# A four-layer transformer program: the masked attention's engines in another order, the key bias as one row, and half of the gate sigmoids computed again

## The chip, the cores and the metric

The program runs on one core of one Trainium2 chip. The metric is the device time in microseconds (us), median of the runs shown; shorter is better. Five engines work side by side, each through its own list of instructions, and meet at semaphores: TensorE (PE in the profile), VectorE (DVE), ScalarE (ACT), GpSimd (POOL) and SyncE (SP), which here issues nearly all DMA transfers.

## The reference, cut to what matters

Two layers follow each other over `x` of 16 sequences x 256 tokens x 512. The first layer is a cross-attention and a gated feed-forward part with quantized activations; the second a masked attention and a feed-forward part with LoRA experts. The change touches the quantized part and the masked attention. In short form, with names of this text:

```
# quantized feed-forward (x1 -> x2)
gate, up  = qdq16(xq @ w_gate.T), qdq16(xq @ w_up.T)      # 16-bit, one scale per tensor: its largest value
sig       = min(round(sigmoid(gate) * 65536), 65535) / 65536
act       = qdq16(gate * sig)                              # scale from the largest |gate * sig|
out       = qdq16(act * up)                                # scale from the largest |act * up|
x2        = x1 + out @ w_down.T

# masked attention (x2 -> x3), one head of width 512; q from layernorm(x2), k from ctx
proj(z)   = (z @ W1.T + b1) @ W2.T + b2
p         = softmax(proj(layernorm(x2)) @ proj(ctx).T / sqrt(512) + mask)   # mask is (256, 256), one for all sequences
x3        = x2 + p @ ctx
```

The kernel folds both projections into one 512 x 512 matrix, so the scores are `norm(x2) @ keys + t + mask`. `keys` is a 512 x 256 array of each sequence. `t` is one number of each key and the same for all queries; it is the key bias of the title.

## The kernel before

Matrices are handled as a high part and a low part in a reduced float format (fp32r), and each product is three matmuls (lines 183 to 185, `product`). The stages run one after the other, each a block with its own tiles; tiles are named by stage: `at_` cross-attention, `pg_` and `pu_` the gate and up projections, `om_` the pass that finds the largest output, `dn_` the down projection, `ma_` the masked attention, `lf_` the last feed-forward part.

**`pu_` (`project`).** 96 tiles of 128 x 512, twelve for each of eight chunks of 512 tokens. For each tile ScalarE takes the sigmoid, VectorE rounds it to 16 bits (`pu_sq`, line 1366), and SyncE stores it to memory (line 1293) and stores the raw up projection beside it.

**`om_` (`output_maximum`).** 48 pieces n of 128 x 1024, six for each chunk. SyncE loads raw up values (512 KB, `om_raw`) and rounded sigmoids (256 KB, `om_sq`). VectorE multiplies gate and sigmoid (`om_prod`, line 1636), ScalarE turns it into the 16-bit `act` in place (line 1576), VectorE multiplies by up (`om_outp`, line 1643) and reduces to the largest (line 1647). Beside this chain the same engines make the keys and key biases of the masked attention. TensorE turns and multiplies; ScalarE takes results out of PSUM (`om_craw`, `om_rout`); GpSimd splits the context in two parts (lines 1673 and 1675), and adds each chunk's bias to the mask for two groups of 128 queries (`key_biases`, line 1682, sixteen adds of 128 x 512 in all). The result, mask plus bias, is stored as `bias_d`, 256 KB for each sequence. GpSimd closes the stage with `partition_all_reduce` (line 1717), which gives the scale that the next stage needs.

**`ma_` (`masked_attention`).** Sequence b passes through: statistics of x2 (DVE), the power for 1/deviation (POOL, line 2007), the shift (DVE, line 2046), normalization (ACT, line 2100), a transposition on TensorE (line 2160), its high part (ACT, 2107) and low part (DVE, 2050), the scores (24 matmuls of 256 columns), the bias and mask and row maximum (DVE `logits`, 2058), the exponentials (ACT, 2128), the transposition of the probabilities (PE, 2181), their parts (ACT 2136, DVE 2063), the product with the values (12 matmuls of 512 columns), and the output (DVE, 2076). Keys and values are split on ACT (2113, 2119) and POOL (2011, 2015). No planner is involved: each engine runs a loop over steps s, written by hand, in which each call carries an offset such as `s + 1` or `s - 2`. The order of the calls in that loop body, and the offsets, are the order of the work.

## Time and profile before

| what | us |
|---|---|
| median of 3 runs | 3729.22 (3728.66 to 3734.64) |
| the profiled execution's own time | 3723.7 |
| its span | 3721.9 |
| PE, DVE, ACT, POOL busy in it | 3253.1, 1929.0, 1532.9, 859.2 |
| granted TensorE clock, mean | 0.942 of full speed |

The span is what the profiler saw; the 1.8 us around it are start and end. The page gives busy time as a share of the whole span, and this program has stages with quite different limits, so the shares are read for one stage at a time. The chain of waits on the page ends in the `lf_` stage and says nothing about the stages of the change.

### The profile page before, as it was taken

The numbers are of one execution on the slowest core, as the hardware profiler recorded it, in microseconds if no ns is written. First come the engines' busy times: TensorE is split into PE (matmuls) and PEld (weight loads), VectorE is DVE, ScalarE is ACT, GpSimd is POOL, SyncE is SP. The second block draws the span as 40 slices with busy tenths as digits, with TensorE's granted clock in tenths as the row PEclk, the third lists the DMA queues.
The fourth block names the chain that finished last, engine by engine and source line by source line (L and its number), as shares of the span: only waits on it lengthen the run. The fifth ranks groups of instructions, "written<-read, shape, count | busy, mean of one in ns | idle before, by whom it ended". The sixth has DMA issues, their size and how long they took to land. (4 is left out here: it accounts for less than half of the span.)

```text
span 3721.9 us, 51622 instructions
## 1 busy us (share of the span) xinstructions
PE 3253.1 (87%) x17272; PEld 2789.6 (75%) x17272; DVE 1929.0 (52%) x3245; ACT 1532.9 (41%) x2915; POOL 859.2 (23%) x1149
## 2 busy tenths in 40 slices
PE   7999899999999969999997859975545999999998
PEld 6998788888888858877874648865533778777776
DVE  3355477777777745557898865534433222222221
ACT  3222276666666633326775656534422111111110
POOL 0000076666766720000004530004310000000000
PEclk9999999999999979999997879997876999999999
DMA  6577654544554435546777874434431001110000
GB/s 178 161 231 231 208 155 141 146 143 141 147 150 133 132 111 206 183 152 226 241 251 232 273 259 158 164 137 151 156 118 62 32 23 34 35 34 32 22 33 12
DMA packets 385410, 524.33 MB, mean 141 GB/s; under 512 B 60435, under 2 KB 245011, under 8 KB 380767
## 3 DMA queue, kind: packets, MB, share of 16 engines
q1 hardware_dynamic: 372424, 512.11, 43.5%
q0 software_dynamic: 2176, 8.39, 0.6%
q10 hardware_dynamic: 10592, 1.04, 0.2%
q8 instruction: 125, 2.05, 0.2%
q14 instruction: 93, 0.75, 0.1%
HBM read 303.29 MB, written 184.55 MB: 131 GB/s over the span
## 5 line engine op out<-in xcount | busy, mean ns | idle before, releaser
L2378 DVE SCALAR_TENSOR_TENSOR lf_hT<-lf_hb,lf_hT 128x512 fp32r<-128x512 f32 x128 | 88.5, 692 | 630.1 <-ACT lf_hT L2436 628.6
L2436 ACT ACTIVATE lf_hT<-lf_hb 128x512 fp32r<-128x512 f32 x128 | 76.6, 598 | 690.6 <-PE lf_py L185 641.7
L766 POOL TENSOR_TENSOR at_prob<-at_prob,at_rec 128x308 f32<-128x308 f32 (+1 forms) x256 | 261.7, 1045 | 265.1 <-DVE at_rec L808 264.8
L901 ACT ACTIVATE at_prob<-at_sc,at_nm 128x77 f32<-128x77 f32 (+1 forms) x1024 | 293.5, 383 | 41.8 <-DVE at_nm L795 41.7
L795 DVE TENSOR_REDUCE at_nm<-at_sc 128x4 f32<-128x308 f32 (+1 forms) x256 | 164.6, 685 | 172.7 <-PE at_sc L955 172.7
L914 ACT ACTIVATE at_pT<-at_tp 128x1024 fp32r<-128x1024 f32 x128 | 131.6, 1028 | 202.1 <-PE at_tp L965 202.1
L183 PE MATMUL lf_hb<-lf_xT,lf_w 128*128 128x512 f32 x512 | 204.1, 399 | 0.0
L184 PE MATMUL lf_hb<-lf_xT,lf_w 128*128 128x512 f32 x512 | 202.5, 395 | 0.0
L184 PE MATMUL lf_py<-lf_w,lf_hT 128*128 128x512 f32 x512 | 202.5, 395 | 0.0
L185 PE MATMUL lf_py<-lf_w,lf_hT 128*128 128x512 f32 x512 | 202.4, 395 | 0.0
L185 PE MATMUL lf_hb<-lf_xT,lf_w 128*128 128x512 f32 x512 | 202.4, 395 | 0.0
L183 PE MATMUL lf_py<-lf_w,lf_hT 128*128 128x512 f32 x512 | 202.3, 395 | 0.0
L183 PE MATMUL dn_py<-qf_wd,dn_om 128*128 128x512 f32 x384 | 150.1, 391 | 38.1 <-DVE dn_om L1858 38.1
L801 DVE TENSOR_REDUCE at_sums<-at_prob 128x4 f32<-128x308 f32 (+1 forms) x256 | 172.7, 675 | 0.0
L183 PE MATMUL pg_bank<-pg_xs,qg_wg 128*128 128x512 f32 x384 | 153.5, 400 | 20.3 <-DVE pg_xs L1359 20.3
L2318 POOL TENSOR_SCALAR lf_var<-lf_mv 128x1 f32<-128x1 f32 x32 | 7.2, 224 | 703.4 <-DVE lf_mv L2331 703.4
L753 POOL TENSOR_TENSOR at_ks<-at_kr,at_ks 128x512 fp32r<-128x512 f32 x128 | 164.8, 1288 | 14.4 <-ACT at_ks L908 14.4
L812 DVE TENSOR_TENSOR at_pT<-at_tp,at_pT 128x1024 fp32r<-128x1024 f32 x128 | 156.1, 1220 | 22.5 <-ACT at_pT L914 22.4
L183 PE MATMUL pu_bank<-pu_xs,qu_wu 128*128 128x512 f32 x384 | 151.0, 393 | 18.1 <-DVE pu_xs L1359 17.5
L183 PE MATMUL at_vq<-at_xT,xo_Wq 128*128 128x256 f32 x512 | 146.9, 287 | 17.4 <-DMA at_xT<-xn_parts 12.6
L183 PE MATMUL at_vq<-at_pT,at_vs 128*128 128x256 f32 x512 | 156.5, 306 | 1.0 <-DVE at_oT L818 0.8
L955 PE MATMUL at_sc<-at_ks,at_qs 128*128 128x256 f32 x1024 | 148.5, 289 | 5.3 <-DMA at_qs<-at_qst 5.2
(315 smaller groups left out, 9635.8 us busy)
## 6 DMA issues: line engine op xcount, KB each, us to landing
at_kr<-k_rows SPq DMA_DIRECT2D x256, 128.0 KB, 2.8
at_qs<-at_qst SPq DMA_DIRECT2D x512, 64.0 KB, 2.0
raw_gate<-pg_stage SPq DMA_DIRECT2D x96, 256.0 KB, 2.0
pu_rg<-raw_gate SPq DMA_DIRECT2D x96, 256.0 KB
raw_up<-pu_stage SPq DMA_DIRECT2D x96, 256.0 KB, 2.1
om_raw<-raw_up SPq DMA_DIRECT2D x48, 512.0 KB, 4.3
dn_raw<-raw_up SPq DMA_DIRECT2D x48, 512.0 KB, 3.8
xn_parts<-pr_xturned SPq DMA_DIRECT2D x32, 512.0 KB, 4.9
```

The source lines that it names most:

```text
L183: pe.matmul(out, lh, rh, start=start, stop=False, **kw)
L184: pe.matmul(out, lh, rl, start=False, stop=False, **kw)
L185: return pe.matmul(out, ll, rh, start=False, stop=stop, **kw)
L753: pool.tensor_tensor(ks[:, n % NK, :, 1, :], kr[:, n % NKR], ks[:, n % NK, :, 0, :].bitcast(F32), ALU.subtract).then_inc(k_low, 1)
L766: ins = pool.tensor_tensor(prob[:, i, :, lo:hi], prob[:, i, :, lo:hi], rec[:, z, g, :].unsqueeze(2).broadcast_to([P, 2 * NTE, hi - lo]), A ...
L795: ins = dve.tensor_reduce(nm[:, n % 2, g, :], sc[n % 2][:, :, lo:hi], AX_X, ALU.max, negate=True)
L801: dve.tensor_reduce(sums[:, z, g, :], prob[:, i, :, SEG[g][0]:SEG[g][1]], AX_X, ALU.add).then_inc(sum_done, 1)
L812: dve.tensor_tensor(pT[:, n % 2, 1], tp[:], pT[:, n % 2, 0].bitcast(F32), ALU.subtract).then_inc(pt_done, 1)
L901: ins = act.activation(prob[:, i, m, lo:hi], sc[n % 2][:, m, lo:hi], ACT.Exp, bias=nm[:, n % 2, g, m:m + 1])
L914: act.activation(pT[:, n % 2, 0], tp[:], ACT.Copy).then_inc(pt_hi, 1)
L955: ins = pe.matmul(sc[n % 2][:, h * NTE + m, :], qs[:, n % NQ, h, m * P:(m + 1) * P], ks[:, n % NK, h, part, :], start=part == 0, stop=part ...
L2378: dve.scalar_tensor_tensor(hT[:, i, 1, :], hb[i][:], 0.0, hT[:, i, 0, :].bitcast(F32), ALU.max, ALU.subtract).then_inc(h_done, 1)
```

## The change

Four parts.

1. **The bias as one row.** `output_maximum` no longer adds the bias to the mask. ScalarE writes the 512 biases of a chunk as one row on one partition, SyncE stores 2 KB for a chunk, and the mask is not loaded there. The masked attention loads the mask once and all biases once (one row of 16 x 256), and TensorE adds the bias to the scores by a matmul of a column of ones with the row: two for each sequence, in plain float32.
2. **Half of the sigmoids.** Pieces with even n of the `om_` pass compute the sigmoid again (ScalarE) and round it again (VectorE, `rounded`). `pu_` stores, and `om_` loads, only those with odd n.
3. **The masked attention's loops.** On each engine the calls come in another order with other offsets, and the outputs are taken one step later (LAG_Y = 3). More buffers: ten for x, three for raw and split keys, four for values.
4. Small: a memset of ones at the start of GpSimd's list in `ma_`; other places for some tiles of `om_`; the last key bias stored one step sooner.

```diff
-                        if gate is not None:
+                        if gate is not None and j % 4 > 1:
                             wait_alone(sp, sq_done, KF * c + j + 3, spacer_s)
                             sp.dma_start(sq_d[...], sq[:, j % 2, :]).then_inc(sq_stored[j % 2], 16)
...
-                    sp.dma_start(sq[:, n % 2, :], part(sq_d, n // SUB, n % SUB)).then_inc(sq_ready[n % 2], 16)
+                    if n % 2:
+                        if n >= 2:
+                            sp.wait_ge(prod_done, n - 1)
+                        sp.dma_start(sq[:, 1, :], part(sq_d, n // SUB, n % SUB)).then_inc(sq_ready, 16)
...
+                def sigmoid(n):
+                    if n >= 2:
+                        act.wait_ge(sq_done, n // 2)
+                    act.activation(sig[:], place(n), ACT.Sigmoid, scale=scal[:, S_G:S_G + 1]).then_inc(sig_ready, 1)
...
-                    act.activation(trow, tb[:], ACT.Identity, bias=bb[:, 0:1]).then_inc(t_out, 1)
+                    act.activation(trow[:, c % 2, :], tb[0:1, :], ACT.Identity, bias=bb[0:1, 0:1]).then_inc(t_out, 1)
+                sigmoid(0)
+                sigmoid(2)
                 for n in range(N):
                     products(n)
+                    if n % 2 and n + 3 < N:
+                        sigmoid(n + 3)
...
+                def rounded(n):
+                    dve.wait_ge(sig_ready, n // 2 + 1)
+                    if n >= 2:
+                        dve.wait_ge(prod_done, n - 1)
+                    dve.tensor_scalar(sq[:, 0, :], sig[:], SIGQ, SIGQ - 1, ALU.mult, ALU.min).then_inc(sq_done, 1)
...
                 for n in range(N):
+                    if n % 2 == 0 and n + 2 < N:
+                        rounded(n + 2)
                     outputs(n)
...
-                for c in range(NCH):
-                    if c + 1 < NCH:
-                        context(2 * c + 2)
-                    if c:
-                        key_biases(c - 1)
-                    if c + 1 < NCH:
-                        context(2 * c + 3)
-                key_biases(NCH - 1)
+                for x in range(2, 2 * NCH):
+                    context(x)
                 pool.wait_ge(row_max, 1)
                 pool.partition_all_reduce(big[:, 0:1], mx_row[:], P, RMAX).then_inc(all_max, 1)
...
-    LEAD_X, LEAD_R, LAG_T, LAG_V = 1, 2, 1, 2
-    NX, NR, NB_ = 8, 2, 3
+    LAG_V, LAG_Y = 2, 3
+    NX, NR, NC, NT_, NB_ = 10, 3, 2, 3, 4
...
# VectorE's loop body of the masked attention
             for s in range(FIRST, LAST + 1):
-                if 0 <= s + LEAD_X < B:
-                    turned_x(s + LEAD_X)
+                if 0 <= s - LAG_Y < B:
+                    outputs(s - LAG_Y)
+                if 0 <= s + 1 < B:
+                    turned_x(s + 1)
+                if 0 <= s + 2 < B:
+                    offset(s + 2)
                 if 0 <= s + 3 < B:
                     statistics(s + 3)
-                if 0 <= s - LAG_T < B:
-                    turned_low(s - LAG_T)
-                    reciprocals(s - LAG_T)
-                if 0 <= s - LAG_V < B:
-                    outputs(s - LAG_V)
                 if 0 <= s < B:
                     logits(s)
-                if 0 <= s + 3 < B:
-                    offset(s + 3)
+                if 0 <= s - 1 < B:
+                    turned_low(s - 1)
+                    reciprocals(s - 1)
# ScalarE's
-                if 0 <= s + LEAD_X < B:
-                    turned_x(s + LEAD_X)
-                if 0 <= s - LAG_T < B:
-                    turned_high(s - LAG_T)
-                if 0 <= s + LEAD_R < B:
-                    keys_high(s + LEAD_R)
+                if 0 <= s + 1 < B:
+                    turned_x(s + 1)
+                if 0 <= s + 2 < B:
+                    keys_high(s + 2)
                 if 0 <= s + 1 < B:
                     values_high(s + 1)
-                if 0 <= s + 3 < B:
-                    normalized(s + 3)
+                if 0 <= s + 2 < B:
+                    normalized(s + 2)
+                if 0 <= s - 1 < B:
+                    turned_high(s - 1)
                 if 0 <= s < B:
                     exps(s)
# TensorE's
+                    pe.matmul(sc[b % 2][:, t, :], ones[:], trow[:, b, :], start=True, stop=False)
                     for k in range(KD):
                         ins = product(...)
...
-                if 0 <= s + LEAD_X < B:
-                    turn_x(s + LEAD_X)
-                if 0 <= s - LAG_T < B:
-                    turn(s - LAG_T)
+                if 0 <= s + 1 < B:
+                    turn_x(s + 1)
                 if 0 <= s < B:
                     scores(s)
+                if 0 <= s - 1 < B:
+                    turn(s - 1)
                 if 0 <= s - LAG_V < B:
                     values(s - LAG_V)
```

What the engines then execute, at three places. First TensorE in the middle of `ma_`, where a step begins (the four probabilities' transpositions are `ma_tp`, the scores `ma_sc`, the values' product `ma_po`). Before:

```order
L185 MATMUL ma_po<-ma_val,ma_pT 128x512
L2160 MATMUL ma_xtp<-ident,ma_xn 128x128 x8
L2181 MATMUL ma_tp<-ident,ma_prob 128x128 x4
L183 MATMUL ma_sc<-ma_rT,ma_xT 128x256
L184 MATMUL ma_sc<-ma_rT,ma_xT 128x256
```

and after:

```order
L185 MATMUL ma_po<-ma_val,ma_pT 128x512
L2166 MATMUL ma_xtp<-ident,ma_xn 128x128 x8
L2176 MATMUL ma_sc<-ma_trow,ma_ones 128x256
L183 MATMUL ma_sc<-ma_rT,ma_xT 128x256
...
L185 MATMUL ma_sc<-ma_rT,ma_xT 128x256
L2188 MATMUL ma_tp<-ident,ma_prob 128x128 x4
L183 MATMUL ma_po<-ma_val,ma_pT 128x512
```

The transposition of the probabilities moved from ahead of the scores to behind them, and a bias matmul stands ahead of each half of the scores.

Then one whole step of VectorE in `ma_`, before:

```order
L2050 TENSOR_TENSOR ma_xT<-ma_xtp,ma_xT 128x1024
L2030 BN_STATS ma_st<-ma_y 128x6 x2
L2035 BN_AGGR ma_mv<-ma_st 128x2 x2
L2040 TENSOR_SCALAR ma_var<-ma_mv 128x2
L2063 TENSOR_TENSOR ma_pT<-ma_tp0,ma_pT 128x512
L2069 RECIPROCAL ma_rec<-ma_sums 128x2
L2076 SCALAR_TENSOR_TENSOR ma_y<-ma_po,ma_rec,ma_y 128x512 x2
L2058 ISA ma_logit,ma_nm<-ma_sc1,ma_bias 128x256
L2058 ISA ma_nm 128x1
L2058 ISA ma_logit,ma_nm<-ma_sc1,ma_bias 128x256
L2058 ISA ma_nm 128x1
L2046 SCALAR_TENSOR_TENSOR ma_shift<-ma_mv,ma_rstd 128x2
```

and after:

```order
L2082 SCALAR_TENSOR_TENSOR ma_y<-ma_po,ma_rec,ma_y 128x512 x2
L2056 TENSOR_TENSOR ma_xT<-ma_xtp,ma_xT 128x1024
L2052 SCALAR_TENSOR_TENSOR ma_shift<-ma_mv,ma_rstd 128x2
L2036 BN_STATS ma_st<-ma_y 128x6 x2
L2041 BN_AGGR ma_mv<-ma_st 128x2 x2
L2046 TENSOR_SCALAR ma_var<-ma_mv 128x2
L2064 ISA ma_logit,ma_nm<-ma_sc0,ma_mask 128x256
L2064 ISA ma_nm 128x1
L2064 ISA ma_logit,ma_nm<-ma_sc0,ma_mask 128x256
L2064 ISA ma_nm 128x1
L2069 TENSOR_TENSOR ma_pT<-ma_tp1,ma_pT 128x512
L2075 RECIPROCAL ma_rec<-ma_sums 128x2
```

The outputs moved ahead of the step (and are those of one sequence earlier); the shift moved from behind the logits to behind the low part of the turned x.

Last, the end of GpSimd's list in `om_`; the first of the two ISA rows has no semaphore to wait for. Before:

```order
L1673 CAST qf_wd<-om_craw 128x4x256
L1675 TENSOR_TENSOR qf_wd<-om_craw,qf_wd 128x4x256
L1682 TENSOR_TENSOR qf_fold<-qf_fold 128x512 x4
L1717 ISA
L1717 ISA big<-om_mx_row 128x1
```

and after:

```order
L1694 CAST qf_wd<-om_craw 128x4x256
L1696 TENSOR_TENSOR qf_wd<-om_craw,qf_wd 128x4x256
L1724 ISA
L1724 ISA big<-om_mx_row 128x1
L1497 UNCONDITIONAL_BRANCH
```

The adds of mask and bias are gone, here the last four.

## Rows read from the trace of the kernel before

**Rows 1.** Busy time in three stages: stretch, its length, engines, clock, DMA share, GB/s.
```profile
460.00:1387.00 927.00, 825.03 (x6037) 776.62 (x6036) 655.50 (x1220) 589.54 (x1603) 605.93 (x929) 0.97 0.47 138
...
1960.00:2215.00 255.00, 187.02 (x760) 139.70 (x760) 207.46 (x150) 150.07 (x167) 116.36 (x64) 0.83 0.81 262
...
2500.00:2760.00 260.00, 147.67 (x768) 132.37 (x768) 112.91 (x240) 98.73 (x161) 86.59 (x48) 0.76 0.42 146
```
**Rows 2.** Scores of `ma_`, by tile: ns min/median/max, first and last start.
```profile
L185 PE MATMUL ma_sc<-ma_rT,ma_xT x128: 274/415/415, 2529.1 to 2738.8; 128*128 128x256 f32 x128
```
**Rows 3.** One step of `ma_` in order of time: start, duration, engine, [idle before, releaser].
```profile
2583.65 1.12 PE L2181 MATMUL ma_tp<-ident,ma_prob 128*128 128x128 f32 x4 [5.39 <-ACT ma_prob L2128]
...
2584.42 0.56 PE L183 MATMUL ma_sc<-ma_rT,ma_xT 128*128 128x256 f32 x1
...
2585.68 1.28 DVE L2030 BATCH_NORM_STATS2 ma_st<-ma_y 128x6 f32<-128x512 f32 x2
...
2587.12 0.28 PE L183 MATMUL ma_sc<-ma_rT,ma_xT 128*128 128x256 f32 x1
...
2587.91 0.69 DVE L2063 TENSOR_TENSOR ma_pT<-ma_tp,ma_pT 128x512 fp32r<-128x512 f32 x1 [0.24 <-issue]
...
2588.55 0.39 PE L183 MATMUL ma_po<-ma_val,ma_pT 128*128 128x512 f32 x1
...
2591.36 1.04 PE L2160 MATMUL ma_xtp<-ident,ma_xn 128*128 128x128 f32 x8
2591.56 1.41 DVE L2076 SCALAR_TENSOR_TENSOR ma_y<-ma_po,ma_rec,ma_y 128x512 f32<-128x512 f32 x2 [2.88 <-PE ma_po L185]
...
2592.76 2.34 POOL L2015 TENSOR_TENSOR ma_val<-ma_cin,ma_val 128x1024 fp32r<-128x1024 f32 x1 [0.42 <-ACT ma_val L2119]
...
2593.57 1.55 DVE L2046 SCALAR_TENSOR_TENSOR ma_shift<-ma_mv,ma_rstd 128x2 f32<-128x2 f32 x1
...
2595.24 1.52 ACT L2100 ACTIVATE ma_xn<-ma_y,ma_shift,ma_rstd 128x512 f32<-128x512 f32 x2 [2.56 <-DVE ma_shift L2046]
...
2597.64 1.00 ACT L2107 ACTIVATE ma_xT<-ma_xtp 128x1024 fp32r<-128x1024 f32 x1
...
2597.79 1.11 PE L2181 MATMUL ma_tp<-ident,ma_prob 128*128 128x128 f32 x4 [5.40 <-ACT ma_prob L2128]
...
2598.68 1.23 DVE L2050 TENSOR_TENSOR ma_xT<-ma_xtp,ma_xT 128x1024 fp32r<-128x1024 f32 x1 [3.56 <-ACT ma_xT L2107]
```
**Rows 4.** The shift of `ma_`, by line: ns min/median/max.
```profile
L2046 DVE SCALAR_TENSOR_TENSOR ma_shift<-ma_mv,ma_rstd x16: 156/1547/2199, 2517.7 to 2709.1; 128x2 f32<-128x2 f32 x16
```
**Rows 5.** Matmuls whose operands are plain float32 (two records for each), by line.
```profile
L1752 PE MATMUL om_rb<-qf_fold x32: 592/592/1061, 2004.1 to 2018.8; 128*128 128x512 f32 x32
```
**Rows 6.** Rounding of a sigmoid tile in `pu_`, by tile.
```profile
L1366 DVE TENSOR_SCALAR pu_sq<-pu_sig x96: 415/417/430, 1684.0 to 1953.1; 128x512 uint16<-128x512 f32 x96
```
**Rows 7.** `om_`, by line: count, busy us, mean ns, idle us before and releaser.
```profile
L1636 DVE TENSOR_TENSOR om_prod<-qf_gate,om_sq 128x1024 f32<-128x1024 int16 x48 | 80.1, 1670 | 29.4 <-DMA om_sq<-gate_sigmoids 29.4
L1643 DVE TENSOR_TENSOR om_outp<-qf_gate,om_up 128x1024 f32<-128x1024 int16 x48 | 74.9, 1561 | 7.0 <-DVE om_mx L1647 1.0
L1647 DVE TENSOR_REDUCE om_mx<-om_outp 128x1 f32<-128x1024 f32 x48 | 58.0, 1208 | 0.1
...
L1682 POOL TENSOR_TENSOR qf_fold<-qf_fold 128x512 f32<-128x512 f32 x16 | 27.7, 1754 | 21.1 <-DMA key_biases<-qf_fold 13.5 <-ACT qf_fold L1597 7.7
```
**Rows 8.** VectorE in `om_`: two starts of `om_prod`, four pieces apart.
```profile
2100.59 3.10 DVE L1636 TENSOR_TENSOR om_prod<-qf_gate,om_sq 128x1024 f32<-128x1024 int16 x1 [2.35 <-DMA om_sq<-gate_sigmoids]
...
2122.31 3.18 DVE L1636 TENSOR_TENSOR om_prod<-qf_gate,om_sq 128x1024 f32<-128x1024 int16 x1 [2.61 <-DMA om_sq<-gate_sigmoids]
```
**Rows 9.** The end of `om_` in order of time.
```profile
2201.40 0.20 DVE L1657 TENSOR_REDUCE om_mx_row<-om_mx 128x1 f32<-128x48 f32 x1
2202.01 2.48 POOL L1682 TENSOR_TENSOR qf_fold<-qf_fold 128x512 f32<-128x512 f32 x2 [13.46 <-DMA key_biases<-qf_fold]
...
2210.41 0.38 POOL L1717 PARTITION_ALL_REDUCE big<-om_mx_row  x1 [5.92 <-issue]
```

More of the change, by code:

```diff
@@ L1444, in output_maximum @@
         raw_ready = [ph.sem(f"raw_ready{i}") for i in range(2)]
-        sq_ready = [ph.sem(f"sq_ready{i}") for i in range(2)]
+        sq_ready, sig_ready, sq_done = ph.sem("sq_ready"), ph.sem("sig_ready"), ph.sem("sq_done")
         up_ready, prod_done, gate_ready, out_done, max_done = (
@@ L1463, in output_maximum @@
         cT = [wd[:, :, 2 * KD:3 * KD, :], wd[:, :, KD:2 * KD, :]]
-        mask = w2[:, 0, :].rearrange("p (q s) -> p q s", q=NK)
-        trow = w2[:, 1, :]
-        bias = w2[:, 2:4, :]
+        trow = w2[0:1, 0:2, :]
+        gb = wd[:, 1, 2:4, :].rearrange("p a (k n) -> p a k n", k=KD)
         betas = rout[:, 0, :].rearrange("p (k n) -> p k n", k=KD)
@@ L1471, in output_maximum @@
         tb = ph.ps("tb", [P, CT])
[L1472 removed]
+        w2_ready, w1_ready, b_ready, c_ready = (ph.sem(n) for n in ("w2_ready", "w1_ready", "b_ready", "c_ready"))
         turned, turned_out, m_full, m_out, beta_full, beta_out, g_full, g_out, gc_full, gc_out = (
@@ L1520, in store_bias @@
                 def store_bias(c):
-                    sp.wait_ge(bias_done, NK * c + NK)
-                    for b in range(NB):
-                        sp.dma_start(bias_d[NB * c + b], bias[:, :, b * S:(b + 1) * S]).then_inc(bias_stored, 16)
+                    sp.wait_ge(t_out, c + 1)
+                    sp.dma_start(bias_d[c:c + 1, :], trow[:, c % 2, :]).then_inc(t_stored[c % 2], 16)
                 def load_down(parts, ks):
@@ L1539, in _ @@
                     if n == 6:
-                        sp.wait_ge(turned, KD)
-                        sp.dma_start(mask, a["fside_1xSxS2_0"].rearrange("o (m p) s -> p (o m) s", p=P)).then_inc(mask_ready, 16)
                         load_context(1)
@@ L1546, in _ @@
                         store_keys(*keys_due(n - 3))
-                    if bias_due(n - 4) is not None:
-                        store_bias(bias_due(n - 4))
+                    if bias_due(n - 3) is not None:
+                        store_bias(bias_due(n - 3))
                     if n == 24:
@@ L1551, in _ @@
                         load_down((0,), (0, KD))
-                for n in range(N, N + 8):
+                for n in range(N, N + 4):
                     if keys_due(n - 3):
@@ L1557, in _ @@
                         load_down((0, 1), (2 * KD, 3 * KD))
-                    if bias_due(n - 4) is not None:
-                        store_bias(bias_due(n - 4))
-                sp.wait_ge(bias_stored, 16 * B)
+                    if bias_due(n - 3) is not None:
+                        store_bias(bias_due(n - 3))
+                sp.wait_ge(t_full, NCH)
+                for s in t_stored:
+                    sp.wait_ge(s, 16 * NCH // 2)
                 load_down((1,), (0, KD))
-                sp.wait_ge(t_full, NCH)
                 load_down((0, 1), (KD, 2 * KD))
@@ L1675, in context @@
                     pool.tensor_tensor(cT[c % 2][:, 1, :, lo:lo + S], craw[:], cT[c % 2][:, 0, :, lo:lo + S].bitcast(F32), ALU.subtract).then_inc(c_low, 1)
-                def key_biases(c):
-                    pool.wait_ge(t_out, c + 1)
-                    if c:
-                        pool.wait_ge(bias_stored, 16 * NB * c)
-                    for q in range(NK):
-                        pool.tensor_tensor(bias[:, q, :].rearrange("p (b s) -> p b s", b=NB), mask[:, q, :].unsqueeze(1).broadcast_to([P, NB, S]),
-                                           trow.rearrange("p (b s) -> p b s", b=NB), ALU.add).then_inc(bias_done, 1)
                 pool.memset(betas, 1.0).then_inc(cleared, 1)
@@ L1703, in _ @@
                 pool.wait_ge(gbraw_done, 1)
+                pool.wait_ge(turned, KD)
                 pool.tensor_copy(gb[:, 0], gbraw).then_inc(gb_hi, 1)
@@ L1923, in masked_attention @@
         rraw = ph.sb("rraw", [P, NR, KD, S])
-        rT = ph.sb("rT", [P, 2, 2, KD, S], F32R)
-        cin = ph.sb("cin", [P, NR, NK, D])
+        rT = ph.sb("rT", [P, NT_, 2, KD, S], F32R)
+        cin = ph.sb("cin", [P, NC, NK, D])
         val = ph.sb("val", [P, NB_, 2, NK, D], F32R)
-        bias = ph.sb("bias", [P, NB_, NK, S])
+        mask = ph.sb("mask", [P, NK, S])
+        trow = ph.sb("trow", [1, B, S])
+        ones = ph.sb("ones", [1, P])
         logit = ph.sb("logit", [P, 2, NK, S])
@@ L1965, in load_values @@
             def load_values(b):
[L1966 to L1973 removed]
+                if b >= NC:
+                    sp.wait_ge(v_low, b - NC + 1)
+                sp.dma_start(cin[:, b % NC], rows(ctx_in, b)).then_inc(c_ready[b % NC], 16)
             def store(b):
@@ L1998, in _ @@
             for i in range(NX):
-                sp.wait_ge(stored[i], 16 * (B // NX))
+                sp.wait_ge(stored[i], 16 * len(range(i, B, NX)))
         @block.gpsimd
@@ L2057, in logits @@
                 for t in range(NK):
-                    dve.tensor_tensor_reduce(logit[:, b % 2, t, :], sc[b % 2][:, t, :], bias[:, b % NB_, t, :], -1.0, 3.0e38, ALU.add, ALU.min,
+                    dve.tensor_tensor_reduce(logit[:, b % 2, t, :], sc[b % 2][:, t, :], mask[:, t, :], -1.0, 3.0e38, ALU.add, ALU.min,
                                              nm[:, b % 2, t:t + 1]).then_inc(max_done, 1)
```

87 lines of the change are left out of this document (43 added, 44 removed).

## The prediction

> **What bounds the kernel now.** I read the busy time by stage first, since the whole-span shares mix stages. In `ma_` (260 us) TensorE is busy 148 us, VectorE 113, ScalarE 99, GpSimd 87 [rows 1]: no engine is even at 60%, the DMA share is 0.42, and the clock is 0.76 of full. So this stage is bound by a circle of waits. `om_` (255 us) is different: VectorE is busy 207 us and the DMA share is 0.81 [rows 1]. The stages before, between and after are left as they are or are bound by TensorE.
>
> The timeline of one step shows the circle [rows 3]. TensorE ends its step with the values' product and the transposition of x at about 2592.4, then idles 5.4 us until the exponentials of the same step are there. These wait in ScalarE's list behind the normalization, that waits 2.56 us for the shift, and the shift stands behind VectorE's outputs and logits, which come after TensorE's last matmul. So TensorE (2583.65 to 2592.4), VectorE (2591.56 to 2595.12) and ScalarE (2595.24 to 2597.64) work in turn: one step is 14.1 us here. Over the stage, sixteen steps' scores run from about 2528.7 to 2738.8 [rows 2]; less the last block of scores, about 4.5 us, that is 205 us for 15 steps, 13.7 us each.
>
> Two things make the circle longer than its work. Behind the 5.4 us of idle, the clock is low: the first 12 score matmuls take 2.70 us (2584.42 to 2587.12), the next 12 take 1.43 us [rows 3], so 1.3 us a step. And the shift, two numbers for each partition, takes 1.55 us, where its shortest is 0.156 us [rows 3, 4]. It starts at 2593.57 inside GpSimd's subtraction (2592.76 to 2595.10) and ends 0.02 us after it: it was held by that subtraction.
>
> **The masked attention, step by step.** After the change the transposition of the probabilities is behind the scores, and the outputs are those of three steps back, so each engine has work of other sequences in hand. Then the longest single list, or a shorter circle, sets the step.
>
> TensorE, at the pace of full clock: x turned 1.04; scores 24 x 0.119 = 2.86; values from 2588.55 to 2591.36, 2.81; probabilities turned, half of x's, 0.5 [rows 3]. Added are the two bias matmuls. A plain float32 matmul leaves two records, 592 ns each at 512 columns, against 390 ns for an fp32r one [rows 5, 3]. The 256-column records of rows 3 take 0.28 for 0.119 of pace, so about 0.16 is latency; 0.43 for 512 columns, 0.215 for 256, and four records are 0.86 us a step. The bounds are 0.24 us (two records at the fp32r pace) and twice 0.86 at the low clock. I take 0.86, the nearest row. Sum: 8.1 us.
>
> VectorE: outputs and logits 2.01 (2591.56 to 2593.57), low part of x 1.23, statistics 2.0 (2585.68 to 2587.91, less 0.24 of waiting), low part of the probabilities 0.69, shift and reciprocal 0.16 each [rows 3, 4]. Sum 6.25 us, if nothing holds it.
>
> Now who waits for whom, counted from the end of a shift. VectorE: statistics to 2.0, logits to 2.7, probabilities and reciprocal to 3.55, outputs to 4.9. ScalarE: normalization to 1.5, the high part of the probabilities to 2.1, the exponentials wait for the logits and run 2.8 to 3.8, then the high part of x to 4.8 (normalization and exponentials are 2.40 together, the high part 1.00 [rows 3]). VectorE's low part of x: 4.9 to 6.1. In the meantime ScalarE did the high part of the next keys, another 1.0, to about 5.8, and GpSimd's subtraction for them starts at 5.9, just ahead of the shift. The subtraction takes 2.34 (as the one for the values [rows 3]), so the shift ends at 8.3 to 8.4. With some tenths for semaphores and one small VectorE operation that may be held by the second subtraction, 8.7 us a step. That is above TensorE's 8.1, so TensorE idles about 0.6 us a step. In the cross-attention it is busy 825 of 927 us (89%) and the clock is 0.97 [rows 1]; so I take full clock.
>
> The trace shows that the shift was held, and nothing of VectorE with an operand in PSUM. The Trainium skill, "SBUF — State Buffer", section "Who interferes with whom", says that VectorE with two SBUF inputs and GpSimd reading SBUF exclude each other for the whole instruction, whoever starts first. By that rule the trace agrees, and the shift is the only large risk in the list above: the outputs, the low parts and the logits each read one operand from PSUM. If the lock fell otherwise (shift first), the step would be TensorE's 8.1; that is the first rival.
>
> Saved: 15 x (13.7 - 8.7) = 75 us. The start stays: GpSimd's first power comes late there and the two transpositions and first scores still follow it. The added wait of TensorE, for mask and bias row, is ahead of its whole list, but both loads are issued with the first x and land while it waits for the power anyway. The end gets shorter, since the last exponentials and transposition no longer wait for a normalization or a transposition ahead of them: about 4 us, between 0 and 8. Memory traffic is four transfers of 0.52 MB a step; at 8.7 us 241 GB/s, less than the 262 of `om_` [rows 1], so I cost it at nothing; if that cover is gone, the step grows (a rival).
>
> **The pass for the largest output.** Removed from GpSimd: 16 adds, 27.7 us [rows 7]. They count by what they hold on VectorE. `om_prod` has a mean of 1670 ns and `om_outp` 1561; the unheld ones take about 1220, nearly the reduction's 1208, which is never held [rows 7]. So VectorE is held (450 + 341) ns x 48 = 38 us, by all of GpSimd's work; the adds are a quarter of its 116 us, 8 to 9 us. Also removed: for the second half of the pass, half of the sigmoid loads and 4 MB of bias stores. VectorE waits 29.4 us for sigmoids [rows 7]; once every four pieces it is 2.4 to 2.6 us, at 21.7 us for four [rows 8]. Some 15 us of the 29.4 lie at the start, where the weights' loads are in front and one odd piece still needs its load: 1 us less. Of the rest I take half, 7 us; bounds 0 and 15.
>
> Added on VectorE: 24 roundings of 1024 columns. The row shows 417 ns for 512 [rows 6]; twice that, 0.83, is the upper end, and 0.417 plus half a reduction's slope (0.27), 0.68, the value taken, as 417 is less than the reduction needs for 512 columns. 24 x 0.68 = 16 us on the engine that bounds the pass, the last rival doubling it. The Trainium skill's same section says that a `tensor_scalar` can take the second port pair too and then excludes GpSimd. No row here shows one beside GpSimd; by that rule a rounding can be held for a whole subtraction, up to 2.4 us, by the other it is never held. I add 4 us, in between. Sigmoids on ScalarE, 24 of at least 1.0 us (its operations of 1024 columns in rows 3), run in the 105 us in which it is idle [rows 1]. Loop: -8 - 7 - 1 + 16 + 4 = +4 us; bounds -16 and +30.
>
> The tail gains. VectorE has its row maximum at 2201.6; GpSimd then still does the last adds (it waited 13.46 us for a store to free the tile) and ends at 2204.5; the all-reduce starts 5.92 us behind that, waiting for nothing shown [rows 9]. After the change nothing but the earlier context work stands ahead, and the ISA row that precedes the all-reduce has no wait, so these 5.9 us pass long before. The scale comes at about 2202.3 instead of 2210.8: 8 us, and `dn_` starts with it, if its loads follow; bounds 0 and 9. In `pu_` TensorE bounds, and the halved stores change nothing.
>
> **Sum.** -75 - 4 + 4 - 8 = -83 us. On the profiled execution's 3723.7 us: 3641. The median of the runs, 3729.2, is 5.5 above it, and one of the three runs is another 5 above; I forecast the median: 3646 us.
>
> **The rivals.**
> - *The shift is not held.* ScalarE's keys come later or the shift slips in first; the step is TensorE's 8.1: 15 x 0.6 = 9 us less, 3637. For it: the race is decided by 0.2 us. Against: at 8.1 the circle has little slack.
> - *The clock dips in each step.* TensorE's short idles bring back the 1.3 us of rows 3: 9.4 a step, +10 us, 3656.
> - *Another wait in `ma_`.* Loads that now come at 241 GB/s, or a buffer freed late (values have only two raw ones, keys three), hold a step at 11 us: +35 us, 3681. For it: loads are issued by one queue behind stores. Against: most are issued a step ahead.
> - *The pass gets worse.* Roundings cost the upper price and are held, and the idle for loads stays: +30 instead of +4, 3672.
> - *Slower than before.* TensorE stays at the low clock, as behind its idles now: its list is then twice 8.1, 16.2 us a step, against 13.7: 15 x 2.5 = +38, with -4 - 4 for the rest, 3759. It decides from a mean step of 14.3 us on. Against: TensorE would then never idle, and in rows 3 the clock rose after 3 us of unbroken work.
> - *The order doesn't loosen the circle.* The step stays at 13.7; only the other parts count, -4 us or so: 3725.
>
> **How the numbers follow.** Forecast (8.4 to 9.0 a step) 40%; shift not held 17%; clock dips 14%; other wait 13%; pass worse 9%; slower 4%; circle stays 3%. The likeliest is 3646. The range 3624 to 3685 takes in the first five but their ends: below, the unheld shift with the pass's lower bound; above, the slow loads. About 0.2% (7.5 us) is what a measurement of this kernel can tell from no change: faster 0.94, same 0.02, slower 0.04.
>
> **What would show it.** In the changed profile: the `ma_` stage near 180 us with a clock above 0.9; the wait of TensorE for the exponentials gone; a shift with a median near 2 us, and starts of it 8.7 us apart; bias matmuls as four records a step. In `om_`: no GpSimd adds, the all-reduce under 1 us behind VectorE's last reduction, roundings of 0.7 us, and VectorE's wait for sigmoids near 15 us. I am wrong if the step is over 9.7 us, or if `om_` grows by more than 15 us.

## The result and the profile after

The changed kernel takes 3639.31 us (median of 4 runs, 3638.54 to 3642.45) against 3728.94 us for the kernel before (4 runs, 3722.93 to 3734.64): a ratio of 0.9761, 95% interval 0.9745 to 0.9778. The profiled execution took 3638.5 us, with a span of 3636.9 and a mean clock of 0.953. The forecast was 3646 us, so the time was right within 7 us, and 4.7 of these come from the 5.5 us added for the median, which lies only 0.8 us above the profiled execution here. By its number alone the result is nearer to the rival "the shift is not held" (3637 us); the trace decides against that rival, since every shift was held. The reason was right for the largest part and wrong in one step that happened to cost little.

Where the 85 us between the two spans (3721.9 and 3636.9) lie, by starts of named instructions in the two traces:

| stretch | before | after | change | forecast |
|---|---|---|---|---|
| up to VectorE's row maximum in `om_` | 2201.40 | 2198.20 | -3.2 | +4 |
| from there to the first product of `dn_` | 22.8 | 16.3 | -6.5 | -8 |
| from there to the first statistics of `ma_` | 280.3 | 281.5 | +1.3 | 0 |
| `ma_`, first statistics to last output | 251.4 | 173.3 | -78.2 | -79 |
| the rest | 965.9 | 967.6 | +1.6 | 0 |

Busy time in the two stages of the change, then in 60 us of steady `ma_` steps (stretch, length, PE, PEld, DVE, ACT, POOL, clock, DMA share, GB/s); it answers to [rows 1]:

```profile
1955.00:2205.00 250.00, 182.78 (x760) 136.87 (x760) 223.92 (x183) 174.97 (x191) 86.33 (x50) 0.85 0.71 225
2490.00:2675.00 185.00, 146.64 (x832) 119.15 (x832) 130.18 (x240) 96.38 (x161) 87.06 (x49) 0.87 0.53 184
...
2560.00:2620.00 60.00, 60.00 (x365) 49.15 (x364) 57.22 (x107) 41.65 (x72) 38.10 (x21) 1.00 0.74 248
```

The last row is the surprise. TensorE is busy all of 60 us at full clock, and VectorE 57.2 of them. The prediction had VectorE set the step and TensorE idle 0.6 us of it.

One step of the changed `ma_` in order of time, answering to [rows 3] (start, duration, engine, instruction, [idle before, releaser]):

```profile
2578.29 2.40 POOL L2016 TENSOR_TENSOR ma_rT<-ma_rraw,ma_rT 128x1024 fp32r<-128x1024 f32 x1 [2.87 <-ACT ma_rT L2119]
2578.45 2.26 DVE L2052 SCALAR_TENSOR_TENSOR ma_shift<-ma_mv,ma_rstd 128x2 f32<-128x2 f32 x1
...
2580.05 0.60 PE L2188 MATMUL ma_tp<-ident,ma_prob 128*128 128x128 f32 x4
...
2583.28 1.03 PE L2166 MATMUL ma_xtp<-ident,ma_xn 128*128 128x128 f32 x8
...
2584.25 0.69 PE L2176 MATMUL ma_sc<-ma_trow,ma_ones 1*128 1x256 f32 x2
...
2586.49 0.69 PE L2176 MATMUL ma_sc<-ma_trow,ma_ones 1*128 1x256 f32 x2
...
2586.97 2.25 DVE L2052 SCALAR_TENSOR_TENSOR ma_shift<-ma_mv,ma_rstd 128x2 f32<-128x2 f32 x1
...
2588.66 0.60 PE L2188 MATMUL ma_tp<-ident,ma_prob 128*128 128x128 f32 x4
```

No row of TensorE has an idle in front: the wait of 5.39 us for the exponentials is gone. TensorE's step is 2580.05 to 2588.66, 8.61 us; VectorE's (one shift to the next) is 8.52. The shift starts 0.16 us behind GpSimd's subtraction of the keys (2578.29 to 2580.69) and ends with it (2580.71), as the prediction had it. Half of the scores takes 2584.25 to 2586.49, 2.24 us; 12 score matmuls at 0.119 are 1.43, so a bias matmul takes 0.81 us out of the list and not 0.43. That is 0.8 us a step more than priced. From start to start the list is 0.96 for turning x, 4.41 for the scores with both biases, 0.36 for turning the probabilities and 2.88 for the values: 8.6 us.

All sixteen shifts, answering to [rows 4]:

```profile
L2052 DVE SCALAR_TENSOR_TENSOR ma_shift<-ma_mv,ma_rstd x16: 2185/2254/2264, 2509.8 to 2638.2; 128x2 f32<-128x2 f32 x16
```

The first of them lies in the start of the stage. Before the change it was not held, now it is:

```profile
2517.69 0.16 DVE L2046 SCALAR_TENSOR_TENSOR ma_shift<-ma_mv,ma_rstd 128x2 f32<-128x2 f32 x1 [11.16 <-POOL ma_rstd L2007]
```
```profile
2509.80 2.19 DVE L2052 SCALAR_TENSOR_TENSOR ma_shift<-ma_mv,ma_rstd 128x2 f32<-128x2 f32 x1 [11.72 <-POOL ma_rstd L2012]
```

`om_` by line, answering to [rows 7] (count | busy us, mean ns | idle before, releaser):

```profile
L1654 DVE TENSOR_TENSOR om_prod<-qf_gate,om_sq 128x1024 f32<-128x1024 int16 x48 | 91.3, 1903 | 12.4 <-DMA om_sq<-gate_sigmoids 12.4
L1661 DVE TENSOR_TENSOR om_outp<-qf_gate,om_up 128x1024 f32<-128x1024 int16 x48 | 64.9, 1353 | 3.3
...
L1644 DVE TENSOR_SCALAR om_sq<-om_sig 128x1024 uint16<-128x1024 f32 x24 | 17.6, 734 | 3.5 <-ACT om_sig L1572 3.5
```

And the end of `om_`, answering to [rows 9]:

```profile
2198.20 0.20 DVE L1678 TENSOR_REDUCE om_mx_row<-om_mx 128x1 f32<-128x48 f32 x1
2198.54 0.38 POOL L1724 PARTITION_ALL_REDUCE big<-om_mx_row  x1 [23.05 <-DVE om_mx_row L1678]
2198.96 0.16 DVE L1681 TENSOR_TENSOR scal<-scal 128x1 f32<-128x1 f32 x1 [0.55 <-POOL big L1724]
...
2213.35 1.15 ACT L1841 ACTIVATE dn_up<-dn_raw,scal 128x1024 int16<-128x1024 f32 x1 [18.08 <-DMA dn_raw<-raw_up]
2214.53 1.23 DVE L1863 TENSOR_TENSOR dn_prod<-qf_gate,dn_up 128x1024 f32<-128x1024 int16 x1 [14.54 <-ACT dn_up L1841]
```

The all-reduce follows the row maximum by 0.34 us, where it took 9.0 before. The scale is there 8.7 us earlier relative to the maximum; `dn_` takes 6.5 of them. In both traces its first operation waits for a load last, and from the issue of that load to the operation it is 6.3 us before (2216.79 to 2223.06) and 8.9 us after (2204.43 to 2213.35).

### The profile page after: what moved, and what is told of

It reads as the page before. It is cut to its first block and busy times, and to the rows that moved or that the text cites. A ratio compares the mean times of both kernels' runs of the same rounds, so it can differ in the third digit from the quotient of the medians.

```text
span 3636.9 us, 51541 instructions
## 1 busy us (share of the span) xinstructions
PE 3247.5 (89%) x17336; PEld 2773.5 (76%) x17336; DVE 1961.0 (54%) x3269; ACT 1554.9 (43%) x2939; POOL 828.2 (23%) x1134
## 5 line engine op out<-in xcount | busy, mean ns | idle before, releaser
L753 POOL TENSOR_TENSOR at_ks<-at_kr,at_ks 128x512 fp32r<-128x512 f32 x128 | 164.8, 1288 | 16.2 <-ACT at_ks L908 16.2
L812 DVE TENSOR_TENSOR at_pT<-at_tp,at_pT 128x1024 fp32r<-128x1024 f32 x128 | 156.1, 1220 | 22.8 <-ACT at_pT L914 22.8
```

Source lines behind the costliest of these rows:

```text
L753: pool.tensor_tensor(ks[:, n % NK, :, 1, :], kr[:, n % NKR], ks[:, n % NK, :, 0, :].bitcast(F32), ALU.subtract).then_inc(k_low, 1)
L812: dve.tensor_tensor(pT[:, n % 2, 1], tp[:], pT[:, n % 2, 0].bitcast(F32), ALU.subtract).then_inc(pt_done, 1)
```

## The experiments

Theory T, read off the trace above: TensorE's list of 8.6 us sets the step. Theory V, the prediction's: VectorE's list with the held shift does. Each kernel was timed beside the kernel before; ratios are compared, and 0.001 is 3.7 us. One ratio is known to about 0.0015, so a difference of two below 0.002 (8 us) is not clear of noise; where such a small one is read below, it rests on the traces. "`ma_`" is the time from the start of the first statistics to the start of the last pair of outputs in its trace. A step is taken from one first transposition of the probabilities to the next, in the steady part of the stage; for the two kernels whose steps differ much the mean of all 15 stands.

| kernel | median us | ratio, 95% interval | `ma_` us | steady step us |
|---|---|---|---|---|
| before | 3723.3 to 3730.6 | 1 | 251.4 | 13.4 mean |
| changed | 3639.3 | 0.9761 (0.9745 to 0.9778) | 173.3 | 8.61 |
| changed, again | 3638.9 | 0.9759 (0.9741 to 0.9776) | 173.7 | 8.61 |
| bias in fp32r, 64 rows | 3634.5 | 0.976 (0.9747 to 0.9774) | 172.1 | 8.51 |
| shift early | 3632.9 | 0.9753 (0.974 to 0.9766) | 169.0 | 8.61 |
| both of these | 3625.3 | 0.9734 (0.9721 to 0.9748) | 160.8 | 7.98 |
| all sigmoids loaded | 3637.3 | 0.9759 (0.9746 to 0.9773) | 174.2 | 8.61 |
| fp32r bias of 128 rows, shift early | 3619.6 | 0.9704 (0.9691 to 0.9718) | 152.4 | 7.22 |
| bias matmuls twice | 3653.1 | 0.98 (0.9784 to 0.9817) | 188.9 | 9.46 |
| bias row alone | 3755.8 | 1.0068 (1.0053 to 1.0084) | 294.2 | 16.2 mean |
| order alone | 3645.3 | 0.9776 (0.9761 to 0.9791) | 168.1 | 8.50 |
| 128 rows, first power early | 3614.3 | 0.9691 (0.9676 to 0.9705) | 140.5 | 7.22 |
| and selector at the head | 3614.7 | 0.969 (0.9673 to 0.9706) | 137.1 | 7.22 |
| and tiles at 32 bytes | 3602.4 | 0.9673 (0.966 to 0.9687) | 137.2 | 7.24 |

**Bias in fp32r, 64 rows.** The biases lie on partitions 0 to 15 (high part) and 32 to 47 (low part); a selector with ones in rows b and 32 + b picks a sequence's.

```diff
-                    pe.matmul(sc[b % 2][:, t, :], ones[:], trow[:, b, :], start=True, stop=False)
+                    pe.matmul(sc[b % 2][:, t, :], sel[:, b, :], bT[:], start=True, stop=False)
```

> The changed kernel, but the key bias goes to the scores as a high and a low fp32r part, by one fp32r matmul for each half (a 64-row selector times 64 rows of biases) where two plain float32 records stood. Theory T (read off the changed kernel's trace: TensorE's list of 8.6 us sets the step, because a bias matmul costs 0.81 us and not 0.43): the list falls to 8.6 - 1.6 + 2 x 0.12 = 7.2 us, TensorE idles, and VectorE's list of 8.5 us, which the held shift makes so long, takes over: 1.5 us less in all (0 to 4). Theory V (the prediction's: VectorE sets the step already): no change at all, and TensorE's idle only grows. The time hardly tells them apart; the trace does: by T the changed kernel had no idle of TensorE and this one has 1.2 us of it a step.

The step went to VectorE's 8.51 and TensorE idled, which the waits of TensorE between 2530 and 2660 us show (total us, times, longest):

```profile
PE ma_xtp L2178 <- ACT ma_xn L2115: 7.3, 11, 3.0
```

In the changed kernel no such row exists. So T: this edit moved the limit from TensorE to VectorE. The idle is 0.5 us a step and not the 1.2 expected, a first sign that the fp32r bias matmul costs more than 0.12.

**Shift early.**

```diff
+                if 0 <= s + 2 < B:
+                    offset(s + 2)
                 if 0 <= s + 1 < B:
                     turned_x(s + 1)
-                if 0 <= s + 2 < B:
-                    offset(s + 2)
```

> The changed kernel, but VectorE makes the shift ahead of the low part of x and not behind it, 1.2 us before GpSimd's subtraction of the keys starts. Both theories: the shift is held no more (0.16 us in place of 2.2). Theory V: VectorE set the step and TensorE idled, so the step falls from 8.6 to TensorE's priced 8.1: 15 x 0.5 = 7.5 us less. Theory T: TensorE's list stays 8.6 us: no change, within 2 us, and VectorE now idles 2 us a step.

```profile
L2052 DVE SCALAR_TENSOR_TENSOR ma_shift<-ma_mv,ma_rstd x16: 143/150/2183, 2514.8 to 2637.6; 128x2 f32<-128x2 f32 x16
```

The median shift fell from 2254 to 150 ns with nothing changed but its place, and VectorE's busy time in 60 us from 57.2 to 42.6; the step stayed 8.61. That shows both that the shift was held by the subtraction it overlapped, and that this did not set the step. V is out. The 4 us that the stage gained lie in its first steps, where TensorE still waits (the second transposition of x follows the first by 6.35 us instead of 8.08).

**Both.**

> Both edits, bias as one fp32r matmul and early shift. Theory T: neither list is above 7.2 us (TensorE) and 6.5 us (VectorE) any more, the step falls by about 1.3 us, 15 x 1.3 = 19 us less than the changed kernel. Theory V: as the early shift alone, or 15 x 0.9 = 13 us with TensorE's priced list of 7.5. Rival: the loads. Four transfers of 0.52 MB in 7.3 us are 287 GB/s, more than any stage showed (262); held to 262, the step is 8.0 and the gain 9 us.

The step is 7.98 us, which is the rival's number: 8.0 for loads at 262 GB/s. But TensorE is busy 60.00 of 60 us, so the loads do not hold it; the agreement was chance. Its list had been priced too short again. One half of the scores in this kernel:

```profile
2581.24 0.38 PE L2188 MATMUL ma_sc<-ma_bT,ma_sel 64*128 64x256 f32 x1
2581.55 0.39 PE L183 MATMUL ma_sc<-ma_rT,ma_xT 128*128 128x256 f32 x1
2581.77 0.28 PE L184 MATMUL ma_sc<-ma_rT,ma_xT 128*128 128x256 f32 x1
...
2583.17 0.38 PE L2188 MATMUL ma_sc<-ma_bT,ma_sel 64*128 64x256 f32 x1
```

It takes 1.93 us, 0.50 more than twelve score matmuls: 0.31 to the next start and 0.22 to the one after, where the pace is 0.12, and another 0.09 ahead of the next bias matmul.

**128 rows.** The same kernel with `braw`, `bT` and `sel` of 128 rows, the rest of them zero.

> As the kernel with the fp32r bias and the early shift, but selector and biases have 128 rows (the added ones zero) where they had 64. There one half of the scores took 1.93 us, 12 x 0.119 = 1.43 and 0.50 more, though only one matmul of 256 columns was added. Theory R: the 0.38 us above a matmul's 0.119 come from the change of the number of rows between neighbours; with 128 rows throughout they go, TensorE's list falls from 7.98 to 7.2 us, and the time by 15 x 0.76 = 11 us. Theory O: they come with any change of operands or of the tile, 128 rows change nothing. Rival of R: VectorE, ScalarE or the loads (280 GB/s would be needed, the highest stage so far moved 262) hold the step above 7.2.

```profile
2564.06 0.36 PE L2188 MATMUL ma_sc<-ma_bT,ma_sel 128*128 128x256 f32 x1
2564.26 0.28 PE L183 MATMUL ma_sc<-ma_rT,ma_xT 128*128 128x256 f32 x1
...
2565.69 0.28 PE L2188 MATMUL ma_sc<-ma_bT,ma_sel 128*128 128x256 f32 x1
2565.81 0.28 PE L183 MATMUL ma_sc<-ma_rT,ma_xT 128*128 128x256 f32 x1
```

Now the bias matmul runs at the pace of its neighbours (0.12 us; the first of a step, right behind the transpositions of x, takes 0.20, as a score matmul in that place does in the order alone), the step is the 7.22 expected, and the ratio falls by 0.003, 11 us. Theory R holds for 64 rows: such a matmul between neighbours of 128 costs 0.38 us on top of its own time. The stage moved 294 GB/s in 60 steady us, so 262 was no ceiling. The Trainium skill ("TensorE: Matmul & The Clock Gate", "Why this matters for your kernels") says that a single matmul of 32 rows takes the same time as one of 128. No run here times one alone; between neighbours of 128 rows the 64-row one takes 0.50 us where the 128-row one takes 0.12.

**Bias matmuls twice.** The column of ones is 0.5, and each matmul is issued twice in a row.

> The changed kernel, with every bias matmul in plain float32 issued twice, each with a column of 0.5 in place of 1. It prices one such matmul by the total: 32 more of them. At 0.62 us each (its start to the next matmul's start in the changed kernel's trace) 20 us more; at 0.81 (with the slower pace behind it counted too) 26 us; at the prediction's price of 0.43, 14 us; at 0.12 (pace of the fp32r ones), 4 us.

The total rose by 0.004 (15 us), 0.46 us for each of the 32 added, and a half of the scores from 2.24 to 2.67 us, 0.43. So the prediction's price of 0.43 was right for the matmul itself. What was missing is the 0.38 around it, the same for plain float32 (0.81 - 0.43) and fp32r (0.50 - 0.12), and paid once for two in a row. That it comes from the number of rows is shown for the fp32r matmul of 64 rows; for the plain float32 one of 1 row the equal size speaks for it, and no run pads that one to 128.

**All sigmoids loaded.** The second part of the change undone in `pu_` and `om_`.

> The changed kernel, but all rounded sigmoids are stored and loaded as before (no sigmoid and no rounding in the pass for the largest output). By the prediction's terms the pass gets shorter: 24 roundings of 0.68 (16 us) and 4 us of holds go, 8 us of waiting for loads comes back: 12 us less than the changed kernel. By the trace of the changed kernel: VectorE waited 12.4 us for sigmoids where it was 29.4 before; if the halved loads did that, 17 us of waits come back and 16 + 4 go: 3 us less (-8 to +4).

No difference (0.9759 against 0.9761 and 0.9759): against the first expectation (-12 us), inside the second (-8 to +4). The waits for sigmoids went back from 12.4 to 30.1 us, and 17.6 us of roundings with 3.5 of waiting for sigmoids disappeared; the operations of `om_prod` and `om_outp` lost 6.6 us net of being held:

```profile
L1633 DVE TENSOR_TENSOR om_prod<-qf_gate,om_sq 128x1024 f32<-128x1024 int16 x48 | 77.6, 1617 | 30.1 <-DMA om_sq<-gate_sigmoids 30.1
L1640 DVE TENSOR_TENSOR om_outp<-qf_gate,om_up 128x1024 f32<-128x1024 int16 x48 | 72.0, 1500 | 7.0 <-DVE om_mx L1644 1.0
```

**Bias row alone.** The changed kernel with the order of the masked attention and the sigmoids as before.

> The kernel before with the bias as one row and nothing else of importance: old order of the masked attention's loops, all sigmoids loaded. The prediction's terms: -8 (GpSimd's adds hold VectorE no more), -8 (tail), and its 0.86 us of bias matmuls a step now in the circle: +13: 3 us less than before. With the measured price of 0.81 us each, and more at the low clock that this order has: 15 x 1.6 to 2.0 = +24 to +30, -10 at the tail and nothing for the adds: 14 to 20 us slower than before.

It is slower than before by 25 us by its ratio (28 by the medians), more than either expectation. `om_` and its tail gained: the first statistics of `ma_` come 10.4 us earlier. `ma_` takes 42.8 us more. In the same stretch of before and of this kernel:

```profile
2560.00:2740.00 180.00, 114.89 (x622) 103.89 (x621) 82.93 (x177) 74.75 (x124) 66.13 (x35) 0.81 0.43 146
```
```profile
2560.00:2740.00 180.00, 135.66 (x543) 106.95 (x541) 60.79 (x160) 64.84 (x110) 54.44 (x31) 0.70 0.33 114
```

The mean clock falls from 0.81 to 0.70, and both halves of the scores now run at the low clock, 0.50 (4.0 and 3.9 us, where before the second took 1.43). So the bias matmuls cost 2.8 us a step in the old circle, not 1.6. The mean step of 16.2 us is the number of the "slower" rival, but only half its mechanism: the clock is low through the scores as it had it, while TensorE still idles 4 us in each step and runs most of the values at full clock. In the changed kernel TensorE has no idle in the steady steps, and the clock there is full.

**Order alone.** The kernel before with the new order and buffers of `ma_`, and the old bias: 256 KB for each sequence, no bias matmul.

> The kernel before with the new order, offsets and buffers of the masked attention and nothing else: GpSimd still adds bias and mask, and 256 KB of it are loaded for each sequence. TensorE's list has no bias matmul (about 7.0 us), VectorE's 8.5 us with its held shift sets the step: 15 x (13.7 - 8.5) = 78 us less than before. Rival: five loads and stores, 2.36 MB in 8.5 us, are 277 GB/s; held to the 262 of the pass for the largest output a step takes 9.0: 70 us less.

It gives -83 us by its ratio (expected -78), with VectorE setting the step as in theory V: TensorE busy 50.5 of 60 us, VectorE 57.2. The order alone is nearly the whole change. Bias row and sigmoids together add 6 us of gain by the medians, which is not clear of noise. In the traces the first statistics of `ma_` come 12.7 us earlier in the changed kernel, 6.9 of them between row maximum and first product of `dn_` (the tail) and 6.3 ahead of the row maximum, and `ma_` is 5 us longer.

```profile
2560.00:2620.00 60.00, 50.46 (x336) 44.25 (x336) 57.16 (x107) 41.78 (x72) 38.39 (x22) 1.00 0.78 260
```

**The changed kernel again.**

> The changed kernel once more, unedited, beside the two below and on the same chip. Its time should be 0.976 of before's again, and its trace shows how much the stages scatter from one execution to the next: the code of the pass for the largest output is the same in it and in the kernels with another bias or shift.

The same ratio (0.9759). Its row maximum in `om_` is at 2197.85; over ten traces with the same code up to there it lies between 2194.4 and 2205.8 (mean 2199.2). Two with all sigmoids loaded and no adds have 2198.5 and 2196.7, two with the adds (before and order alone) 2201.4 and 2204.5. So no single comparison of this place between two traces shows less than some 10 us.

**First power early.**

```diff
+                pool.memset(warm[:], 1.0).then_inc(warmed, 1)
+                pool.wait_ge(warmed, 1)
+                pool.tensor_tensor(warm[:], warm[:], warm[:], ALU.pow).then_inc(warmed, 1)
                 with pool.Fori(0, NCH // 2) as it:
```

> As the fp32r bias of 128 rows with the early shift, and GpSimd takes a power of two dummy columns at the head of the down projection, where it is idle for 60 us. Theory L: the 10.8 us between the first variance and GpSimd's first power in the masked attention, in which it waits for nothing that the trace shows, belong to the first power behind a reduction over partitions, as the 5.9 us ahead of the reduction did the other way round; done once ahead, they go, and the time falls by 8 to 10 us. Rival: they belong to the start of a stage or to the wait itself, and nothing changes.

GpSimd's first power of the masked attention, in the changed kernel and in this one:

```profile
2508.92 0.73 POOL L2012 TENSOR_TENSOR ma_rstd<-ma_var,neghalf 128x2 f32<-128x2 f32 x1 [16.71 <-issue]
```
```profile
2216.70 0.75 POOL L1826 TENSOR_TENSOR dn_warm<-dn_warm 128x2 f32<-128x2 f32 x1 [11.71 <-issue]
...
2506.77 0.72 POOL L2020 TENSOR_TENSOR ma_rstd<-ma_var,neghalf 128x2 f32<-128x2 f32 x1 [6.08 <-DVE ma_var L2054]
```

The 11.7 us now pass in `dn_`, and the power follows the variance by 0.2 us where it took 10.8: theory L, and `ma_` is 11.9 us shorter. That it is the reduction ahead which brings them is argued: each time it was the first power behind the program's reductions, but not the first of the program, whose powers run from 165 us on. The Trainium skill ("GPSIMD Engine Reference", "Instruction dispatch") puts the first call of freshly loaded code at about 6 us without a row of its own; the trace before the change agrees for the all-reduce (5.92 us), while this one takes nearly twice that. But the total fell only by 0.0013, 5 us, which is within the noise: the chunks of `dn_` are now 33.6 us apart instead of 32.6, and that takes back 7 us between the first product of `dn_` and the first statistics of `ma_` (281.9 and 289.0 us).

**Selector at the head.**

> As the kernel with the early first power, and VectorE makes the selector (2048 columns, 2.3 us) at the head of its list in the masked attention, where it waits 12 us for x, and not between the second and the third sequence's statistics. If that place was on the path of the start, 2 us less; if the start still waits for GpSimd or a load, nothing.

`ma_` is 3.4 us shorter, so that place was on the path; the total is the same, and the difference is below what the medians can tell.

**Tiles at 32 bytes.** The time of a matmul of 512 columns in `dn_` is 0.227 us from start to start without the dummy tile and 0.233 with it, and TensorE is busy all of 250 us there (2230 to 2480) in both. What had changed is that an 8-byte tile stood ahead of the others.

```diff
# down projection
-        warm, warmed = ph.sb("warm", [P, 2]), ph.sem("warmed")
         raw = ph.sb("raw", [P, 2, SC])
...
         y = ph.sb("y", [P, 2, NT, D])
+        warm, warmed = ph.sb("warm", [P, 2]), ph.sem("warmed")
# masked attention, last feed-forward part
         shift = ph.sb("shift", [P, 2, NK])
+        ph.sb("pad", [P, 2])
...
         rstd = ph.sb("rstd", [P, 2])
+        ph.sb("pad", [P, 4])
```

> As the kernel with the selector at the head, and only addresses in SBUF are changed: the tile of two columns of the down projection (8 bytes a partition) comes behind its other tiles instead of ahead of them, and pads of 8 and 16 bytes are put behind the small tiles of the masked attention and of the last feed-forward part, so that all operands of matmuls start at a multiple of 32 bytes. Theory A (address): in the down projection the pace of matmuls of 512 columns rose from 0.227 to 0.233 us when the 8 bytes came; it falls back, 8 us less; the last part has the 0.233 too and some 3400 such matmuls: 0.0066 x 3400 = 22 us less, the masked attention 1 to 2; 31 us in all. Rival: the pace comes from something else in those stages (GpSimd's dummy power, the operands' values, power): nothing changes.

Half right. In `dn_` the pace is 0.227 again and the chunks are 32.6 us apart: that is the address, since the dummy power is still there and nothing else changed. In the masked attention and the last part nothing moved: 0.233 stayed. The gain is 6 us and not 31; by the medians it would be within noise, and the trace shows it (288.7 us and now 282.1 between the first product of `dn_` and the first statistics of `ma_`). With a ratio of 0.9673 this kernel is the fastest of all, 0.0087 (32 us) below the changed one.

## Why the prediction was right, and where not

- **The circle and its loosening** (-75 and -4): right, -78.2 measured. From the first scores to the last sequence's, 206.4 us became 128.5, 77.9 less, and the end behind them lost 3.9. But "the start stays" was wrong: from the first statistics to the first scores it takes 27.7 us where it took 24.0. The first shift, held 2.19 us and not 0.16, is 2.0 of these 3.7. Order alone gives nearly all of the gain.
- **The held shift**: right in place, length and cause: it starts 0.16 us behind the subtraction in every step, takes 2.25 us, and takes 0.15 when moved. VectorE's list, put at 8.3 to 8.4, is 8.51; the small operation that might be held by the second subtraction is the variance, 0.63 us where it took 0.17. With the rule of the Trainium skill ("SBUF — State Buffer", "Who interferes with whom"), that VectorE with two SBUF inputs and GpSimd reading SBUF exclude each other for a whole instruction, these traces agree.
- **"That is above TensorE's 8.1, so TensorE idles about 0.6 us a step"**: wrong. The list is 8.61. Twice 0.38 us around the bias matmuls is missing; the matmuls' own price was right, and the rest of the list about 0.2 us too high (7.21 in the sum; 6.98 by the 7.22 us of the kernel with 128 rows less its two matmuls of 0.12). It cost nothing because the two lists tie within 0.1 us, and because "some tenths" had been added to VectorE's. That the step came out so near to 8.7 is luck: the list that was to set it is 8.51, and the one that sets it had been put 0.5 us too low.
- **GpSimd's adds** (-8): right as far as VectorE's operations show it. Without the adds, and with all sigmoids loaded, `om_prod` and `om_outp` are held 30 us (bias row alone) and 32 (all sigmoids loaded) instead of 38, by the same measure of 1220 ns for an unheld one. In the time of the whole pass it is not seen above the scatter.
- **Waits for sigmoids** (-8 in all): too small, -17. At the start 15.0 us of waiting became 10.6, and of the 14.4 us behind it 1.8 are left, where half had been taken.
- **Roundings** (+16 and +4): 17.6 us, 0.73 each (20.8 and 0.87 in the second trace). An unheld one takes 0.68, as priced. The few that began more than 0.1 us before the end of a GpSimd operation ended some 0.5 us behind it and took 1.3 to 1.8 us, so they can be held, as the first of the prediction's two rules had it; but only 2 of 24 met one here and 5 in the second trace. The holds on `om_prod` and `om_outp` rose too, from 30 and 32 us to 39 and 35. Together the second part of the change is worth nothing that the medians can tell: what the waits give, the roundings and holds take. The forecast of +4 for the loop and the measured -3 differ by less than the scatter of the row maximum (11 us over ten traces of the same code).
- **The tail** (-8): -8.7 up to the scale, of which 2.2 are given back to the first load of `dn_`, as the condition "if its loads follow" had left open.
- **Clock**: 1.00 in the steady steps, as predicted. Over the whole stage (2490 to 2675) it is 0.87 and not above 0.9, the sign that had been named: from 2496 to 2530, where TensorE is busy only 10 of 34 us, it is 0.50. Low clock through both halves of the scores, the slower rival's condition, came only where the bias matmuls were put into the old order.

## What to carry to other kernels

Where two engines' lists tie within some tenths of a microsecond, shortening either alone gives next to nothing: here 0 and -3 us alone, both within noise, -10 together, and -21 with the 128 rows that the traces then pointed to. A time that matches a rival's number is not yet that rival: the 7.98 us step agreed with "loads at 262 GB/s", and TensorE's busy time, 60.00 of 60 us, refuted it. And before a small matmul is put between large ones, try it with their number of rows: here the zeros cost nothing, and the change of shape did.

## What the runs showed of the hardware that was not expected

- A matmul of 64 rows (fp32r) or of 1 row (plain float32) between neighbours of 128 costs 0.38 us beyond its own time at full clock; the fp32r one with 128 rows costs its 0.12 alone.
- GpSimd's first power behind a reduction over partitions came 10.8 us after its operands (10.3 in the kernel before), with no row in the trace; a dummy power in a stage where GpSimd is idle took that time out of the way, and followed its own operands by 11.7 us.
- A VectorE `tensor_scalar` from float32 to 16 bits, both in SBUF, that began inside a GpSimd subtraction took 1.3 to 1.8 us instead of 0.68.
- Moving the tiles of the down projection by 8 bytes slowed the matmuls of 512 columns there by 3% on the mean (0.227 to 0.233 us). The masked attention and the last part have about 0.233 with and without pads. Which address matters, and whether theirs can reach 0.227, stays open; it was not tried further.
